# Expert-major router logits turned back by transposes, batch 1's projections moved among the first maxima, and epsilon as an activation bias

## The reference, cut to what matters

```python
x = x + 0.5 * ffn(layernorm(x)); x = x + attention(layernorm(x)); x = x + 0.5 * ffn(layernorm(x))

def ffn(x, gate_w, w_gate, w_up, w_down):       # x: 4 x 1024 x 128, 8 experts, inner width 512
    affinity = softmax(einsum('bsd,ed->bse', x, gate_w)).transpose(0, 2, 1)
    gating, idx = top_k(affinity, 256)          # per batch and expert
    x_in = x[bidx, idx]
    h = silu(x_in @ w_gate) * (x_in @ w_up)
    return zeros_like(x).at[bidx, idx].add(gating[..., None] * (h @ w_down))

def attention(x, ...):                          # 16 heads of width 8, q and k turned by a 3d rope
    q, k, v = x @ Wq + bq, x @ Wk + bk, x @ Wv + bv
    return softmax(rope(q) @ rope(k).T * 8 ** -0.5) @ v @ Wo + bo
```

## Time and profile before

| what | value |
|---|---|
| runs | 1208.99, 1209.43, 1207.38 us; median 1208.99 |
| profiled execution | 1207.35 us, its span 1205.3 us |
| busy, share of the span | PE 90%, DVE 76%, ACT 64%, POOL 50% |
| mean granted TensorE clock | 0.94 of full |
| first mixture, turn to the attention, groups, second mixture | about 0 to 298, 298 to 362, 362 to 968, 968 to 1205 us of the span |

### The profile page before, as it was taken

One profiled execution on the slowest core, in us unless ns is written; L12 is line 12 of the kernel. 1 busy time (PEld: TensorE's weight loads), 2 busy tenths in 40 slices (PEclk: granted clock), 3 DMA queues, 4 the chain that ended last, 5 costly groups with the idle time before them and its releaser, 6 DMA issues.

```text
span 1205.3 us, 23761 instructions
## 1 busy us (share of the span) xinstructions
PE 1088.2 (90%) x8900; PEld 478.3 (40%) x8900; DVE 918.8 (76%) x1510; ACT 769.6 (64%) x1461; POOL 600.1 (50%) x619
## 2 busy tenths in 40 slices
PE   6199999898599999999999999999998889999993
PEld 6167666565132222222222222222222256666762
DVE  5745855465979999999999999999997554854441
ACT  3054322432368999999989999899999836222220
POOL 4046888775378511100003447455430187677886
PEclk6579999999598999999999999999999988999997
DMA  9025456458514220212111222112310125345553
GB/s 274 32 60 115 91 112 136 88 118 198 135 37 123 61 64 19 58 46 58 40 29 40 52 52 62 25 40 58 81 45 8 31 79 130 83 92 101 114 101 30
DMA packets 93065, 93.95 MB, mean 78 GB/s; under 512 B 14684, under 2 KB 70108, under 8 KB 92920
## 3 DMA queue, kind: packets, MB, share of 16 engines
q1 hardware_dynamic: 70424, 75.66, 22.6%
q0 software_dynamic: 22528, 16.79, 10.3%
HBM read 64.22 MB, written 30.13 MB: 78 GB/s over the span
## 4 chain that ended last, share of the span: by engine, by line
DVE 43%; PE 35%; issue 11%; POOL 5%; ACT 4%; DMA 1%; SPq 0%; DVEq 0%; POOLq 0%; another core or an unknown queue 0%; ACTq 0%
DVE mx L1877 38%; PE pA L1329 7%; PE pS L1317 7%; POOL out_dram L655 3%; ACT Pt L1154 3%; PE pO L1318 3%; PE pS L1318 3%; PE pO L1469 3%; DVE ge L1564 2%; PE pS L1490 2%; PE pA L1297 2%; PE pS L1235 2%; POOL xg L632 1%; PE pA L1405 1%; PE pA L1235 1%
## 5 line engine op out<-in xcount | busy, mean ns | idle before, releaser
L1877 DVE TENSOR_REDUCE mx<-pA 128x2 f32<-128x1024 f32 x512 | 585.2, 1217 | 13.8 <-PE pA L1405 13.0
L1154 ACT ACTIVATE Pt<-pS 128x512 f32<-128x512 f32 x1024 | 556.3, 596 | 30.9 <-PE pS L1490 25.0
L1469 PE MATMUL pO<-Pt,Vst 128*16 128x256 f32 x4096 | 321.5, 386 | 12.5 <-ACT U L1145 12.5
L1049 ACT ACTIVATE Pt<-pS 128x512 f32<-128x512 f32 x128 | 76.4, 597 | 199.9 <-PE pS L1317 176.6
L632 POOL DMA_INDIRECT xg<-zd,idx x128 | 128.4, 1003 | 149.4 <-DVE idx L1684 76.3
L1405 PE MATMUL pA<-Kst,Qst 48*128 48x512 bf16 x704 | 140.9, 397 | 20.1 <-DVE mx L1877 18.9
L1469 PEld LDWEIGHTS pO<-Pt,Vst 128*16 128x16 f32 x4096 | 68.0, 94 | 204.3 <-issue 107.2
L1317 PE MATMUL pS<-Pt,wg 128*128 128x512 f32 x256 | 139.7, 628 | 4.5 <-DVE Pt L1711 2.1
L1490 PE MATMUL pS<-Qst,Kst 51*128 51x512 bf16 x704 | 138.6, 390 | 5.1 <-issue 1.0
L722 POOL TENSOR_TENSOR mparts<-mx,onesm 128x32 bf16<-128x32 f32 x16 | 4.0, 252 | 267.1 <-DVE mx L1882 210.9
L1329 PEld LDWEIGHTS pA<-wd,Pt 128*128 128x128 f32 x960 | 113.5, 192 | 16.8 <-issue 16.8
(11 more groups left out here) (229 smaller groups left out, 1214.7 us busy)
## 6 DMA issues: line engine op xcount, KB each, us to landing
wg<-w_gate_dram SPq DMA_DIRECT2D x32, 256.0 KB
wu<-w_up_dram SPq DMA_DIRECT2D x32, 256.0 KB
wd<-w_down_dram SPq DMA_DIRECT2D x32, 256.0 KB
qk<-parts SPq DMA_DIRECT2D x64, 96.0 KB
Kst<-qk SPq DMA_DIRECT2D x132, 32.0 KB
zd<-Z SPq DMA_DIRECT2D x8, 512.0 KB
vp<-pair SPq DMA_DIRECT2D x4, 1024.0 KB, 4.6
Vst<-vp SPq DMA_DIRECT2D x16, 256.0 KB
```

Source lines behind the costliest of these rows:

```text
L1049: S.activation(sg[:, u % 2, :], pG[u % 2], ACT.Silu).then_inc(s_silu, 1)
L1154: S.activation(Pt[:, s % 4, j, r * 512:(r + 1) * 512], pS[:, bank_of(k, 4 * s + 2 * j + r), :], ACT.Exp, scale=SCALE).then_inc(s_exp, 1)
L1469: last = M.matmul(pO[32 * h:32 * h + 16, cols], Vst[k][:, s % 8, h, :], Pt[:, s % 4, h // 2, (h % 2) * 512 + 256 * a:(h % 2) * 512 + 256 * ...
L1877: V.reduce_max(mx2[:, k, 2 * j:2 * j + 2, c, half], pA[ring[q, a] % 2][:, :, :], AX.X).then_inc(s_Ar, 1)
```

## The change

1. **Logits by expert.** For `hh` = 1 and 3 the 16 products that move `gate_t` are replaced by `logits_by_expert`: `gate_t`, padded with zeros to 32 columns, is the stationary operand, and four products move 512 columns of `ZT` each into four column parts of one bank. ACT copies the bank to SBUF (`by_expert`, the room of `ge`), and `front(hh, 4)` is now four transposes of it, from which DVE takes the maxima with a stride. For `hh` = 3 that front moves from gap 2 of iteration 18 to gap 3.
2. **Batch 1's projections** (`u` = 2 and 3, m = 15 to 24) leave the gaps of iterations 14 and 15 and stand in `window` behind pieces 0, 2, 4, 6 and 8, 10, 12, 13 of group 0. ACT now reads them out with the bias, POOL makes their products with cos and sin and their sums, and ACT makes `high` and `middle` of both in the new place. `store_values(0)` moves behind `store_parts(0)` and the load of weights 15, `store_values(1)` behind the loads of x.
3. **Epsilon** is no longer added on DVE; ACT's square root takes it as its bias (`eps`, set by POOL), and `veps` goes.

```diff
@@ tables()
+    place[1, 4] = ("g", 1)
-    for m in range(5, 25):
+    for m in range(5, 15):
         place[divmod(55 + m, 5)] = ("s", m)
-                           ... (18, 1), (18, 2), (18, 4)] + ...
+                           ... (18, 1), (18, 3), (18, 4)] + ...
+    place[18, 2] = ("g", 3)
-    for u, at in ((4, 22), (5, 28), (6, 32), (7, 37)):
+    for u, ats in ((2, (0, 2, 4, 6)), (3, (8, 10, 12, 13)), (4, range(22, 26)), (5, range(28, 32)), (6, range(32, 36)), (7, range(37, 41))):
@@ SP
             for j in range(11, 15):
                 load_weights(j)
-            store_values(0)
             store_parts(0)
             load_weights(15)
+            store_values(0)
             store_parts(1)
             load(0)
             load(1)
-            store_values(1)
...
                 load_x(b, x1_in)
+            store_values(1)
             store_parts(2)
             store_parts(3)
@@ POOL
             scatter(RUN - 1)
+            product(2, 0)
+            product(2, 1)
+            add_products(2)
+            product(3, 0)
             rest(2)
+            product(3, 1)
+            add_products(3)
+            lowest(2)
             rest(3)
-            lowest(2)
             lowest(3)
@@ ACT
-                S.activation(sd[:, tiles(i)], veps[:, tiles(i)], ACT.Sqrt)
+                S.activation(sd[:, tiles(i)], mv[:, tiles(i), 1], ACT.Sqrt, bias=eps[:, 0:1])
+                if key and key[0] == "g":
+                    act.wait_ge(*written(key))
+                    S.activation(by_expert, sidebank, ACT.Copy).then_inc(s_room, 1)
-            middle(2)
-            middle(3)
...
+            for u in (2, 3):
+                for i in range(4):
+                    projected(u, i)
+                value_rows(u)
+            high(2)
             deviation(6)
+            middle(2)
             deviation(7)
...
             normalise(6)
+            high(3)
             turned_half(0)
             turned_half(1)
+            middle(3)
             normalise(7)
@@ PE
+            def logits_by_expert(hh):
+                bank, sem = open_bank(("g", hh))
+                pe.wait_ge(*was_read(("f", hh, 3)))
+                for g in range(4):
+                    last = M.matmul(bank[32 * g:32 * g + 32, :], gate_t[:, :], ZT[:, g * 512:(g + 1) * 512], start=True, stop=True,
+                                    tile_position=(0, 32 * g))
+                last.then_inc(sem, 1)
@@ DVE, moments
                 link(last)
                 for n in ts:
                     last = V.bn_aggr(mv[:, n, :], stats[:, n % CH, :])
-                link(last)
-                V.tensor_scalar(veps[:, tiles(i)], mv[:, tiles(i), 1], EPS, None, ALU.add).then_inc(s_ve, 1)
+                last.then_inc(s_ve, 1)
```

More of the change, by code:

```diff
@@ L84, in tables @@
     window = {(0, 20): ("T", 0), (0, 21): ("T", 1), (0, 26): ("T", 2), (0, 27): ("T", 3), (1, 4): ("m",)}
-    for u, at in ((4, 22), (5, 28), (6, 32), (7, 37)):
-        for i in range(4):
-            window[divmod(at + i, 32)] = ("PR", u, i)
+    for u, ats in ((2, (0, 2, 4, 6)), (3, (8, 10, 12, 13)), (4, range(22, 26)), (5, range(28, 32)), (6, range(32, 36)), (7, range(37, 41))):
+        for i, at in enumerate(ats):
+            window[divmod(at, 32)] = ("PR", u, i)
     win = {window[at]: i for i, at in enumerate(sorted(window))}
@@ L145, in program @@
         ge = sb("ge", [P, N], BF16)
+        by_expert = ge[:, :].bitcast(F32)
         count = sb("count", [P, 1], F32)
@@ L217, in program @@
         num, den = scr[:, 0:2, :], scr[:, 2:4, :]
-        pairs = {4: (scr[:, 0, :], scr[:, 2, :]), 5: (scr[:, 1, :], scr[:, 3, :]), 6: (room[:, 0, :], room[:, 1, :]),
-                 7: (U[1][:, :], U[2][:, :])}
+        pairs = {u: (scr[:, u % 2, :], scr[:, 2 + u % 2, :]) for u in range(2, 6)}
+        pairs |= {6: (room[:, 0, :], room[:, 1, :]),
+                  7: (U[1][:, :], U[2][:, :])}
         dens = sb("dens", [P, P], F32)
@@ L928, in deviation @@
                 act.wait_ge(s_ve, nth(i))
-                S.activation(sd[:, tiles(i)], veps[:, tiles(i)], ACT.Sqrt).then_inc(s_sd, 1)
+                if i == 0:
+                    act.wait_ge(s_fill, 3)
+                S.activation(sd[:, tiles(i)], mv[:, tiles(i), 1], ACT.Sqrt, bias=eps[:, 0:1]).then_inc(s_sd, 1)
             def normalise(i, first=0, end=CH):
@@ L1202, in front @@
                     if hh:
-                        pe.wait_ge(*was_read(("f", hh, 3)))
-                    for k in range(0 if hh else CH, HT):
-                        if hh == 0 and k % 4 == 0:
-                            pe.wait_ge(*was_read(("f", 0, k // 4)))
-                        last = M.matmul(bank[:, k * E:(k + 1) * E], ZT[:, k * P:(k + 1) * P], gate_t[:, :], start=True, stop=True)
+                        pe.wait_ge(*was_read(("g", hh)))
+                        for k in range(4):
+                            last = M.transpose(bank[:, k * P:(k + 1) * P], by_expert[:, k * P:(k + 1) * P], ident[:, :])
+                    else:
+                        for k in range(CH, HT):
+                            if k % 4 == 0:
+                                pe.wait_ge(*was_read(("f", 0, k // 4)))
+                            last = M.matmul(bank[:, k * E:(k + 1) * E], ZT[:, k * P:(k + 1) * P], gate_t[:, 0:E], start=True, stop=True)
                 elif n < 7:
@@ L1340, in last_down @@
                 pe.wait_ge(s_idx, j + 1)
-                pe.wait_ge(*was_read(("s", 24) if j < RUN else ("f", 3, NF - 1)))
+                pe.wait_ge(*was_read(("s", 14) if j < RUN else ("f", 3, NF - 1)))
                 for i in range(IC):
@@ L1387, in _ @@
                     pe.wait_ge(*was_read(("f", 0, k // 4)))
-                M.matmul(bank_of_use(("f", 0, 4))[:, k * E:(k + 1) * E], ZT[:, k * P:(k + 1) * P], gate_t[:, :], start=True, stop=True)
+                M.matmul(bank_of_use(("f", 0, 4))[:, k * E:(k + 1) * E], ZT[:, k * P:(k + 1) * P], gate_t[:, 0:E], start=True, stop=True)
             for n in range(2, 8):
@@ L1429, in window_use @@
                     if i == 0:
-                        pe.wait_ge(s_winr, win["T", 2 * (b - 2) + 1] + 1)
-                    last = project(op, (wq, wr)[i // 2], 2 * (b - 2) + i % 2, bank)
+                        pe.wait_ge(*(was_read(("s", 4)) if b == 1 else (s_winr, win["T", 2 * (b - 2) + 1] + 1)))
+                    last = project(op, (wq, wr)[i // 2], 2 * (b % 2) + i % 2, bank)
                 else:
@@ L1769, in use @@
                     setup(key[1])
-                else:
+                elif key[0] == "p":
                     add_to_x(key[1], key[2])
```

49 lines of the change are left out of this document (29 added, 20 removed).

## The result

| kernel | runs | median, us | lowest to highest | ratio to before, 95% interval |
|---|---|---|---|---|
| before | 4 | 1208.96 | 1207.38 to 1209.43 | |
| changed | 4 | 1197.25 | 1196.37 to 1198.01 | 0.9905 [0.9888, 0.9922] |
| before, second series | 11 | 1207.43 | 1203.26 to 1212.34 | |
| changed, second series (`e8_changed_again`) | 6 | 1198.65 | 1197.17 to 1200.56 | 0.9930 [0.9907, 0.9952] |

The change makes the kernel 11.7 us faster in the first series and 8.8 us in the second, 1196 to 1201 us over both series, against 1195.1 forecast. The profiled execution of the changed kernel took 1198.01 us with a span of 1196.2, the slowest of its four runs, while that of before, 1207.35, lay under all of its own: the spans are 9.1 us apart.

The account below looks back on a forecast made before the run. No engine bounds it alone; PE bounds the first mixture, DVE the first maxima. Terms -9.7 + 0.5 + 1.0 - 2.3 - 2.2 - 0.7 - 0.5 = -13.9 give 1195.1 us; range 1190 to 1201.

Parts of the forecast that it names:

- Iterations 14 and 15: First mixture: eight projections, two sets of values and a 1.07 us wait leave a PE without gaps; -9.7 us.
- The read-back ahead of group 0: SP's loads before the first piece land at 288.2 to 291.0 against 288.8 wanted; 0 to 2.2, taken as +0.5 us.
- land, taken as 2.7 us: Read-back ahead of group 0: the loads land 2.7 us after they are issued.
- The first rival: The read-back is late: group 0 lands at 290.5 to 291.0, costing 2 more, 1197 us; chance 0.12.
- The projections among the maxima: First maxima of group 0: projections hidden at full clock, values 0.7 over, twice; taken as +1.0 us.
- The rival of the half clock: First maxima: PE at half speed costs 7.4 instead of 1.0, so 1201.5 us; chance 0.10.
- Cost 0: POOL's six added operations, 14.0 us, fit its 21.15 us idle before the first product of `u` = 4.
- Epsilon: DVE's addition removed: 0.7 us gained at the start, 0.5 for three later roots.
- Iteration 2: Logits as four column parts together in 1.2 us instead of 3.5, fewer transposes' time; net -2.3 us.
- Iteration 18: Affinities 2.4 to 3.3 us earlier, PE waits 2.2, half speed costs 1.6; between 0 and 3.3, taken as -2.2.
- signs of being right: Iteration 14's first projection gap to first piece 25.2 us; full clock there; iteration 2 logits 1.2; iteration 19's gather 15 earlier.
- signs of being wrong: First piece waits for a DMA; PE at 0.50 before piece 13; POOL without idle before `u` = 4; longer affinity wait.

Follow-up runs that it names:

- e8_changed_again: The changed kernel, unaltered, run again in a second series; 1198.65 us, ratio 0.9930 to before.
- e3: Batch 1's projections among the first maxima alone, with their SyncE queue and GpSimd operations, on the kernel before; 1206.89 us, ratio 0.9997.
- e5: The changed kernel with GpSimd's fills of Kst moved behind its work on the gains; 1196.72 us, ratio 0.9911 to before.
- e4: The changed kernel with group 0's Q read back before iteration 15's weights, V behind batch 0's last store, K last; 1195.88 us, ratio 0.9904.
- e9: The changed kernel with the edits of e4, e5 and e7 together; 1190.66 us, ratio 0.9863 to before.
- e10: e9 with the affinities' transposes of iteration 18, and following steps up to iteration 20's, one gap later; 1189.44 us, ratio 0.9855 to before.
- e1: Epsilon as the square root's bias alone, on the kernel before; 1207.36 us, ratio 0.9997.
- the three parts alone: The kernel before with one part each: epsilon 0.9997, logits by expert 0.9964, batch 1's projections 0.9997.
- e7: The changed kernel with GpSimd waiting for the shifts of moments 6 and 7 before product(3, 1); 1195.79 us, ratio 0.9908 to before.
- e12: e5 with DVE's addition of epsilon back; 1197.52 us, ratio 0.9921 to before.
- e11: The changed kernel with DVE's addition of epsilon back; 1199.25 us, ratio 0.9930 to before.

## Why the forecast was right, and where it was off

**Iterations 14 and 15** were right, -9.9 for -9.7, in every kernel that has the edit. So was the price of the gap: products that leave a PE without idle time give back their full pitch.

**The read-back ahead of group 0** was mis-sized: +0.5 forecast, +1.8 to +2.1 measured, and 3.3 in e3. The chain was read rightly. The stores started within 0.1 us of the forecast (17.0 us behind compaction 14), took 5.15 us of the 3.9 to 6.7, and the loads began where forecast. The step that failed is "land, taken as 2.7 us": they landed 4.08 us behind V's issue (3.84 in e8, 4.07 in e3). The 2.7 were those of a 96 KB store, and V's load moves 256 KB and was issued last; which of the two makes it late no run separates. And the value taken lay at the low end of the range 0 to 2.2. The first rival, group 0 landing at 290.5 to 291.0, is thus what happened: set against compaction 14 the piece started at 290.7 on the clock of the kernel before. Its reason was worse than its figure: the DMA engines were not full when these loads ran before, but 81% busy from 278 to 283 us and 48% from 283 to 288. Besides, a wait that ends at a DMA has a second price that I counted nowhere here: half clock behind it, 0.8 and 0.9 us until `moments(6)` in the two traces of the changed kernel and up to 2.0 in e5.

**The projections among the maxima** were right at full clock, 15.99 - 15.15 = 0.84 for 1.0, where there is no such wait (e4, e9, e10). The rival of the half clock did not come: the clock was 1.00 from 293 to 303 us, though PE stood idle there three times, for 0.49 to 0.74 us, until DVE had read a bank. The half clock before that, from 288.9 to about 292, came behind the wait for V and not from these stops: in e4 the clock is 1.00 all the way from 286 to 305 us. The rule of the Trainium skill that would have made it the forecast ("TensorE: Matmul & The Clock Gate", "A second HAM failure mode: psum-queue depth-cycling") doesn't hold in this stretch.

**POOL** was priced at nothing, by its idle time alone, and the cover did hold, 2.39 us of it left. What failed is the sentence "Cost 0": POOL's operations hold DVE's. That is +1.78 us for two shifts (0.98 + 1.14 - 2 x 0.17), and it would be 1.8 more with the addition of epsilon in place. The Trainium skill states this ("SBUF — State Buffer", section "Who interferes with whom"): DVE and GpSimd share a pair of ports; a `tensor_scalar` whose operands allow it can use both ports and then contends with any GpSimd instruction, a DVE operation with two SBUF inputs contends with one that reads SBUF, `tensor_reduce` and the form of `tensor_scalar` that writes an accumulator do not; who comes second waits to the end of the other. The traces agree: Z and `veps` are held by fills (4.06 us against 1.11; 0.69 against 0.17), `shift` by products but not by fills (0.17 at 6.46 us), and neither the maxima by products nor the 1.28 us compares by fills. Two rows of the trace before could have priced it. One is the earlier trace rows, 0.69 us for 128x8 numbers. The other is this `shift` of the second mixture:

```profile
996.84 0.98 DVE L1560 SCALAR_TENSOR_TENSOR shift<-mv,rstd 128x8 f32<-128x8 f32 x1
```

It took 0.98 us instead of 0.17 and ended at 997.82, where POOL's two products into Z (2.16 us from 995.64) ended at 997.80.

**Epsilon** had the wrong place. Forecast: 0.7 at the start and 0.5 at the roots, 1.2 in all. Measured: nothing at the start while the fill is there, 0.16 without it; at the roots of `moments(6)` and `(7)` 0.46 alone (e1) and 2.07 with POOL's products beside them. What it saves against those products is more than the forecast said, by a mechanism that the forecast did not have.

**Iteration 2** was right, -2.5 for -2.3: 1.00 us for four column parts of 512 columns. The copy by ACT lay beside the gate and up pair as the order had it, and what the Trainium skill warns of ("TensorEngine Tiling (Array Packing)", section "PSUM Bottleneck") cost nothing there.

**Iteration 18** was mis-sized by my own numbers. The affinities' transposes came 8.89 us behind compaction 19 instead of 11.83, 2.9 earlier (forecast 2.4 to 3.3), PE waited 2.31 (forecast 2.2), and the half clock behind it cost 1.7 (forecast 1.6). 2.9 - 1.7 = 1.2; having written both numbers down I took 2.2, nearer to the gain without its price. In e9 the same wait of 2.30 us was followed by no half clock.

**Why the total held.** By the stages the change brings 8.2 to 8.4 us; the medians say 8.8 and 11.7. Four runs of each kernel made the first difference, and the kernel before spreads from 1202.7 to 1213.2 over 29 runs in another series, 0.9% and not the 0.2% that I took as what can be told. The forecast of -13.9 missed the stages by 5.5 to 5.7 us, and that the range held all the same is in part luck: the range was wide, and the two medians stand 3.3 and 0.4 to 0.6 us beyond what the stages give. The large misses all point one way: 1.3 to 1.6 us at the read-back, 1.8 under POOL's operations, 0.7 to 0.8 at the half clock behind the wait, 1.0 in iteration 18 and 0.8 to 1.2 at the start. Two of the signs of being right say so too: from the place of the first projection in iteration 14 to the first piece 26.6 us (260.46 to 287.04) and not 25.2, and the gather of iteration 19 9.6 us earlier (1021.20) and not 15, a figure that was above the sum itself. And two of its signs of being wrong came: the first piece waited for a DMA (3.24 us), and PE ran at 0.50 before piece 13 (289 to 291 us).

What stays open: the ratios of the three parts alone multiply to 0.9958, 3 to 6 us short of the whole. By the stages 1.6 us of it are epsilon's and POOL's products together (`moments(6)` to T is +3.4 in e3, -0.5 in e1 and +1.3 with both), 1.3 to 1.5 the longer wait for V in e3 and 1.4 the half clock in e3's iteration 2; the rest isn't told apart from the spread. Why the clock falls behind some waits and not behind others of the same length is not known from these runs.

## What to carry to other kernels

Price work moved to an engine with idle time twice: by its own cover, and by what it holds on the engine beside it while it runs. A short operation that takes several times its usual time in the trace, and ends when another engine's does, names the cost. And when a transfer is moved up behind shortened work, time its landing by a transfer of its own size and place in the queue, and add the clock that PE loses if it waits.

## What the runs showed of the hardware

- POOL holds DVE for up to the whole of its operation: an addition on 128x8 numbers took 1.98 us instead of 0.17 (e3), a product of two SBUF operands 1.14 instead of 0.17 (the changed kernel). With POOL kept idle the product takes 0.17 again (e7), and with the fills moved the first addition does (e12).
- Four column parts of 512 columns, moving float32, take 1.00 us of PE; sixteen products of 8 columns took 3.5.
- A wait of PE of 2.3 to 4.5 us is often, not always, followed by half clock: behind the same 2.3 us in iteration 18 the pair took 3.3 us in the changed kernel and 1.7 in e9, and behind 2.82 us ahead of the first piece e11 stayed at full clock. With a wait of 1.1 to 1.2 us ahead of the first piece it never was (e4, e9, e10).
- One stretch with roots took 16.7 to 21.8 us in fourteen traces of nearly the same program.
